# Row statistics taken where a tile is finished, shorter stages between the layers, and two accumulators for the expert outputs

## The reference, cut to what matters

```
x = x + lru(layernorm(x))          # gated complex linear recurrence
x = x + ffn(layernorm(x))          # binarized weight
x = x + ssm(layernorm(x))          # state space scan
x = x + ffn(layernorm(x))          # the same weight again
x = x + attention(layernorm(x))    # 16 heads, x @ Wq.T and so on, out @ Wo.T
x = x + moe(layernorm(x))          # 64 experts, top 8, 256 places each
x = x + linear_attention(layernorm(x))
x = x + moe(layernorm(x))          # the same experts again

layernorm(x)        = (x - mean) / sqrt(var + 1e-5)      # per row
binarize_weight(w)  = (where(w >= 0, 1, -1) * mean(|w|, per row) - w) + w
ffn(x)              = x @ binarize_weight(w).T + bias
moe(x): logits = x @ router.T; the 8 best experts of a row with normalized softmax weights;
        y_row = sum over its experts of weight * (silu(x @ gate) * (x @ up)) @ down
```

## Time and profile before

| | |
|---|---|
| time, median of 3 runs | 5667.46 us (5666.89 to 5673.59) |
| the profiled execution | 5669.14 us, its span 5667.4 us |
| PE busy | 4820.4 us, 85% of the span |
| DVE busy | 2362.7 us, 42% |
| ACT busy | 1644.4 us, 29% |
| POOL busy | 1527.4 us, 27% |
| DMA, mean over the span | 70 GB/s |

### The profile page before, as it was taken

One profiled execution on the slowest core, in us unless ns is written; L12 is line 12 of the kernel. 1 busy time (PEld: TensorE's weight loads), 2 busy tenths in 40 slices (PEclk: granted clock), 3 DMA queues, 4 the chain that ended last, 5 costly groups with the idle time before them and its releaser, 6 DMA issues. The chain is left out here.

```text
span 5667.4 us, 66951 instructions
## 1 busy us (share of the span) xinstructions
PE 4820.4 (85%) x26288; PEld 2581.4 (46%) x26288; DVE 2362.7 (42%) x3233; ACT 1644.4 (29%) x2764; POOL 1527.4 (27%) x951
## 2 busy tenths in 40 slices
PE   6045988789999999985999949999999989589996
PEld 2013433333333333244655626666666654465654
DVE  1754588537666666744211122333333320512111
ACT  2511555120455555732111112222222210211111
POOL 0011000100577777011444430111111110044444
PEclk9567999899999999986999979999999999699998
DMA  1000000000000000013888840000000021368887
GB/s 46 0 9 17 16 0 0 0 32 1 1 1 1 1 1 1 1 55 112 221 224 226 226 87 25 29 23 29 31 29 31 21 101 61 131 172 224 218 225 164
DMA packets 223978, 395.83 MB, mean 70 GB/s; under 512 B 30480, under 2 KB 118544, under 8 KB 223632
## 3 DMA queue, kind: packets, MB, share of 16 engines
q1 hardware_dynamic: 166352, 249.13, 13.1%
q0 software_dynamic: 57344, 142.64, 12.3%
HBM read 288.88 MB, written 107.02 MB: 70 GB/s over the span
## 5 line engine op out<-in xcount | busy, mean ns | idle before, releaser
L2163 PE MATMUL linb_pr_ps<-lin_z,linb_wt 128*128 128x512 f32 x1536 | 677.8, 595 | 16.4 <-POOL linb_slope_own L2133 16.4
L1365 ACT ACTIVATE attc_prob<-attc_ps 128x512 f32<-128x512 f32 x1024 | 549.1, 596 | 443.0 <-PE attc_ps L1276 442.2
L1239 POOL TENSOR_TENSOR attc_acc<-attc_acc,attc_prob 128x2048 f32<-128x2048 f32 x120 | 547.9, 4566 | 121.6 <-ACT attc_prob L1365 109.2
L1389 DVE TENSOR_REDUCE attc_peak<-attc_ps 128x2 f32<-128x1024 f32 x384 | 469.6, 1225 | 258.0 <-PE attc_ps L1284 258.0
L1276 PE MATMUL attc_ps<-att_q,att_k 32*128 32x512 f32 x2048 | 528.6, 616 | 0.0
L1284 PE MATMUL attc_ps<-att_k,att_q 32*128 32x512 f32 x1536 | 450.0, 663 | 0.0
L2163 PEld LDWEIGHTS linb_pr_ps<-lin_z,linb_wt 128*128 128x128 f32 x1536 | 286.1, 191 | 342.1 <-issue 324.8
L2339 DVE SCALAR_TENSOR_TENSOR linb_gated<-linb_osb,linb_norm_w,linb_proj 128x512 f32<-128x512 f32 x64 | 94.4, 1474 | 668.1 <-ACT linb_osb L2266 668.1
L2140 POOL TENSOR_TENSOR linb_sq<-linb_osb 128x512 f32<-128x512 f32 x64 | 70.1, 1095 | 1039.0 <-ACT linb_osb L2266 1039.0
L1297 PE MATMUL attc_ps<-attc_prob,att_v 128*32 128x256 f32 (+1 forms) x3472 | 316.5, 437 | 0.3 <-ACT attc_prob L1365 0.3
L886 DVE TENSOR_TENSOR_SCAN ssmb_state<-ssmb_decay,ssmb_bu 128x2048 f32<-128x2048 f32 x64 | 279.7, 4409 | 78.9 <-ACT ssmb_decay L833 78.9
(11 more groups left out here) (510 smaller groups left out, 7652.8 us busy)
## 6 DMA issues: line engine op xcount, KB each, us to landing
moe1w_wgu<-in_L_ffn_gate_up_proj SPq DMA_DIRECT2D x32, 1536.0 KB
moe2w_wgu<-in_L_ffn_gate_up_proj SPq DMA_DIRECT2D x32, 1536.0 KB
moe1w_wd<-in_L_ffn_down_proj SPq DMA_DIRECT2D x32, 512.0 KB
gated_features<-linb_gated SPq DMA_DIRECT2D x64, 256.0 KB
moe2w_wd<-in_L_ffn_down_proj SPq DMA_DIRECT2D x32, 512.0 KB
linc_gt<-gated_features SPq DMA_DIRECT2D x7, 2048.0 KB
linb_wt<-in_L_attn_b_qkv_w SPq DMA_DIRECT2D x16, 768.0 KB
residual_rows<-residual SPq DMA_DIRECT2D x2, 4096.0 KB
```

Source lines behind the costliest of these rows:

```text
L1239: pool.tensor_tensor(acc[:, n % 2, :, :], before, prob[:, U % NP, :, :], ALU.add).then_inc(pool_done, 2 if at == 1 else 1)
L1365: nc.scalar.activation(prob[:, U % NP, h, :], ps[:, n % 3 if at < 0 else at % 6, :], ACT.Exp).then_inc(exp_done, 1)
L1389: V.tensor_reduce(peak[:, w // TT % 2, i % QH, 2 * hp:2 * hp + 2, b], ps[:, bank:bank + 2, :], axis=AX.X, op=ALU.max).then_inc(mx_used, 1)
L2163: last = nc.tensor.matmul(pr_ps[:, use % 2, :], wt[:, b, kind, k, :], z[:, k, t * NB:(t + 1) * NB], start=(k == 0), stop=(k == DT - 1))
```

## The change

- `g.stats` is a buffer of the whole program. The 16 `bn_stats` leave `Norm`; each is issued on DVE where a tile of `g.X` is finished: while x is loaded (in four DMAs instead of one), after the adds of `lrud`, `ffn1`, `ffn2`, `atte` and `linc`, after the last column block of `ssmb`, and at the end of `moe1c`.
- `project_and_add` has its loops unrolled, reads the features of a tile in place (no copy on ACT), has four PSUM tiles, and PE waits for no bias.
- `lru_outputs` is one stage. `W_out` is loaded during `lruc` into `th[0]`, once `recur(0)` is done. The binarized weight is made within the stage, one DVE step behind each of the first adds, and transposed by PE after tiles 13 and 14.
- To make room in `lruc`, `spare` and `ones` shrink, and `turn` in `gate_and_unwind` works on halves of 1024 columns.
- The ffn bias is loaded in each `ffn` stage.
- The four attention weights come transposed from the host; `attw` is gone, and `atta` loads them.
- Experts 0 and 1 of a pair add to tables of their own, `g.y_dram[0]` and `g.y_dram[1]`; a scatter waits only for the scatters of the same expert number of the pair before. POOL issues the gathers of pair j + 3 ahead of the scatters of pair j - 1, into `NX = 20` buffers. `moe_logits` also writes 4 MB of zeros to the second table. At the end both tables are loaded in four pieces each, DVE sums them, and the second `moe` stores the sums to the output.

```diff
@@ setup @@
+            for j in range(4):
+                sp.dma_start(g.X[:, 4 * j:4 * j + 4, :], ...).then_inc(loaded[j], 16)
...
+        @block.vector
+        def _(dve):
+            for i in range(TT):
+                dve.wait_ge(loaded[i // 4], 16)
+                nc.vector.bn_stats(g.stats[:, i, :], g.X[:, i, :]).then_inc(summed, 1)
@@ Norm.on_vector @@
         for i in range(TT):
-            nc.vector.bn_stats(self.stats[:, i, :], self.X[:, i, :]).then_inc(self.summed, 1)
-        for i in range(TT):
-            dve.wait_ge(self.summed, i + 1)
             nc.vector.bn_aggr(self.mv[:, i, :], self.stats[:, i, :]).then_inc(self.summed, 1)
@@ project_and_add @@
-            pe.wait_ge(loaded, 16)
...
+            for i in range(TT):
+                if i >= NY:
+                    pe.wait_ge(y_used, i - NY + 1)
+                for k in range(DT):
+                    last = nc.tensor.matmul(y_ps[:, i % NY, :], h[:, k, i * P:(i + 1) * P], w[:, k, :], start=(k == 0), stop=(k == DT - 1))
+                last.then_inc(y_ready, 1)
...
+            for i in range(TT):
+                dve.wait_ge(y_ready, i + 1)
+                dve.wait_ge(biased, i + 1)
+                nc.vector.tensor_tensor(g.X[:, i, :], g.X[:, i, :], y_ps[:, i % NY, :], ALU.add).then_inc(y_used, 1)
+                dve.wait_ge(y_used, i + 1)
+                nc.vector.bn_stats(g.stats[:, i, :], g.X[:, i, :]).then_inc(summed, 1)
@@ lru_recurrence @@
+            sp.wait_ge(dve_step, after_vector("recur0"))
+            sp.dma_start(th[0].rearrange("p (k f) -> p k f", f=D), g.dram["L0_attn_a_W_out"].rearrange("(k p) f -> p k f", p=P)).then_inc(w_loaded, 16)
...
-                turn(r, cos_sum[r], sin_sum[r], spare[:, :], gx[r], -1)
+                for c in range(2):
+                    half = slice(c * (T // 2), (c + 1) * (T // 2))
+                    turn(r, cos_sum[r][:, half], sin_sum[r][:, half], spare[:, :], gx[r][:, half], -1, half)
@@ lru_outputs (tensor) @@
+                if i == TT - 3:
+                    pe.wait_ge(bw_ready, 1)
+                    turned(0)
+                    turned(1)
+                elif i == TT - 2:
+                    turned(2)
+                    turned(3)
@@ ffn (vector, in the loop) @@
+                    dve.wait_ge(y_used, i + 3)
+                    dve.sem_inc(passed, 1)
+                    nc.vector.bn_stats(g.stats[:, bass.ds(i, 1), :].rearrange("p o s -> p (o s)"), ...).then_inc(summed, 1)
@@ ssm_scan, add_back @@
+                if e == DT - 1:
+                    dve.wait_ge(added, e * TC + t + 1)
+                    for i in range(t * 4, (t + 1) * 4):
+                        V.bn_stats(g.stats[:, i, :], g.X[:, i, :]).then_inc(stats_ready, 1)
@@ attention @@
-            normalized_features(nc, g, "atta", z)
-            transpose_weights(nc, g, "attw", v, ...)
+            normalized_features(nc, g, "atta", z, tuple(zip(("L1_attn_a_Wq", ...), (*wt, wo))))
@@ moe_logits (sync) @@
+            sp.dma_start(g.y_dram[0][0:T, :].rearrange("(i p) d -> p i d", p=P), g.X[:, :, :]).then_inc(x_saved, 16)
+            sp.wait_ge(blank, 1)
+            for i in range(0, TT, NB_ROWS):
+                sp.dma_start(g.y_dram[1][i * P:(i + NB_ROWS) * P, :].rearrange("(i p) d -> p i d", p=P), nothing[:, :, :]).then_inc(x_saved, 16)
@@ moe_experts @@
-        NX = 16
+        NX = 20
...
+            for r in range(TT // NR):
+                tiles = slice(r * NR, (r + 1) * NR)
+                for to, rows in ((g.X, g.y_dram[0]), (second, g.y_dram[1])):
+                    sp.dma_start(to[:, tiles, :], ...).then_inc(back[r], 16)
+            for r in range(TT // NR):
+                sp.wait_ge(summed, r + 1)
+                if last:
+                    sp.dma_start(g.dram["out"][0, r * NR * P:(r + 1) * NR * P, :]..., g.X[:, r * NR:(r + 1) * NR, :]).then_inc(stored, 16)
...
             def scatter(j, x):
                 mine = [4 * j + 2 * s + x for s in range(2)]
-                others = [4 * j + 2 * s for s in range(2)] if x else [4 * j - 3, 4 * j - 1]
-                for y in others:
-                    if y >= 0:
-                        pool.wait_ge(added[y % NY], 16 * (y // NY + 1))
+                if j >= 1:
+                    for y in mine:
+                        pool.wait_ge(added[(y - 4) % NY], 16 * ((y - 4) // NY + 1))
...
             for j in range(PAIRS):
+                if j + AHEAD < PAIRS:
+                    for n in range(4 * (j + AHEAD), 4 * (j + AHEAD + 1)):
+                        gather(n)
                 if j >= 1:
                     for x in range(2):
                         scatter(j - 1, x)
-                if j + AHEAD < PAIRS:
-                    for n in range(4 * (j + AHEAD), 4 * (j + AHEAD + 1)):
-                        gather(n)
...
+            for r in range(TT // NR):
+                dve.wait_ge(back[r], 32)
+                nc.vector.tensor_tensor(g.X[:, r * NR:(r + 1) * NR, :], ..., second[:, r * NR:(r + 1) * NR, :], ALU.add).then_inc(summed, 1)
+                if not last:
+                    dve.wait_ge(summed, r + 1)
+                    for i in range(r * NR, (r + 1) * NR):
+                        nc.vector.bn_stats(g.stats[:, i, :], g.X[:, i, :]).then_inc(stats_ready, 1)
```

## The result

The changed kernel takes 5481.49 us in the median of 4 runs (5474.49 to 5487.45), beside 5669.05 us for the kernel before (4 runs, 5666.89 to 5673.59). The ratio is 0.9672, with a 95% interval of 0.9658 to 0.9685: faster, by 3.3%. The forecast was 5486 us. The profiled execution has a span of 5480.8 us; before it was 5667.4, so 186.6 us have to be accounted for.

What follows compares the result with a forecast made beforehand. No single engine bounds the whole; POOL's scatter chain through the DMA sets the expert stages. Terms of 220.0 us less and 37.4 more, net -183, take 5669 to 5486 us; 8 in 10 range 5455 to 5535.

Steps and rivals of the forecast that it cites:

- The step that carried half of the sum: Expert stages moe1c and moe2c: POOL's chain through the DMA sets the pace, PE only looks like the bound; -107 us.
- The chain: Expert stages: scatter (0.30 + 1.6 us), landing (8.9), the same for the other expert; about 20 to 21 us a pair.
- rival B: Expert stages: gathers do not come earlier, something unseen holds them, the pace stays 20.5; 5593 us, chance 0.07.
- Rival C: Expert stages: up to four accumulating scatters at once hinder one another, slower than before; 5729 us at 23 a pair, chance 0.03.
- The pace: Middle of moe1c and moe2c: 18.5 us a pair instead of 20.49, ends 18.4 and 19.6; 53.6 us saved in moe1c.
- Rival A: Expert stages: the DMA engines take POOL's place as the bound, 19.2 us a pair; 5524 us, chance 0.20.
- moe1a and moe2a: Routing stages: DVE's tile 4 waits for a store queued behind x and zeros; +5.3 us each, bounds -9.5 to +15.
- Statistics: Six other stages lose 9.51 us of statistics at their head: -57.1 us; they come back where nothing hides them.
- lrud with binarizing: From lruc's end through lrud and binw: 62.7 us instead of 96.0, 33.3 saved, binarizing hidden under PE's products.
- attw: Attention: the stage goes, -18.9 us, and its 4 MB load hides under what is left of atta.
- the ends of the expert stages: Earlier last scatter against loading and adding two tables: +4.3 us for moe1c, +9.5 for moe2c.
- the load of two tables: End of the expert stages: 8 MB instead of 4 MB come, 11.5 us more of data than before.

Runs made afterwards that it cites:

- Run 1: Changed kernel with POOL's old order (scatters ahead of gathers) and 16 gather buffers, the two tables kept: 5470.47 us, ratio 0.9643.
- Run 2: Kernel before with POOL's new order and 20 gather buffers, still one table with chained scatters: 5638.42 us, ratio 0.9939.
- run 8: Changed kernel loading the gate and up weights of each pair's first expert a second time from pair 4 on: 5481.14 us, ratio 0.9666.
- run 9: As run 8, but both experts' gate and up weights are loaded a second time: 5587.55 us, ratio 0.9847.
- run 3: Changed kernel with GpSimd pausing ahead of the ninth gather until the first pair's products have begun: 5469.58 us, ratio 0.9641.
- run 4: Changed kernel with GpSimd's old order but still 20 gather buffers: 5465.74 us, ratio 0.9638.
- run 10: Changed kernel with 28 extra identity products on TensorE behind the product of tile 3 in moe1a and moe2a: 5486.78 us, ratio 0.9672.

## Why the prediction was right, and where it was not

**The bound.** The step that carried half of the sum holds: GpSimd's queue waits in order for landings of its own scatters and sets the pace, while PE looked like the bound. Run 1 cut the chain and left the rest: 18.4 us a pair. Run 2 gave GpSimd a head start and left the chain: the pace went back to 20.5 when the stock was gone.

The chain was drawn one landing too long. Its terms, twice 0.30 + 1.6 + 8.9, make 21.6 us and not "20 to 21", more than the 20.49 found. In the kernel before (GpSimd, timeline; columns as in the earlier trace rows) the second scatter of expert 1 and, four gathers later, the next pair's first scatter are:

```profile
2951.52 1.56 POOL L1864 DMA_INDIRECT residual_rows<-moe1c_ye,moe1w_index  x1 [0.30 <-issue]
2958.50 1.62 POOL L1864 DMA_INDIRECT residual_rows<-moe1c_ye,moe1w_index  x1 [0.30 <-issue]
```

The second may not begin before the first has landed, and it begins after 7.0 us with no idle time beyond the usual 0.30. So this landing took less than 7 us and lay under the four gathers. Only the landing ahead of expert 1's scatters stood open: 8.1 us of idle time in the mean, beside 12.4 us of issuing, 20.5 in all (scatters of pairs 1 to 27). The 8.9 us of the earlier trace rows are those of expert 0's scatters alone, 10 of the 20 in its window. The sum did not suffer, since with the wait gone the pace is PE's 18.4 us however many landings there were; but that the landing times explained the pace "to the microsecond", which the prediction held against rival B, was a coincidence.

Rival B fell with the lead of 33.9 us (I had worked out 40; the pair's results come later in its 18.4 us than I placed them). Rival C fell with up to four scatters at once and pairs of 18.36 us. The second scatter of expert 1 does land later than before, 8.5 us after its issue rather than 5.3 (medians in moe1c, by the semaphore events of the two traces), but nothing waits for it any more.

**The pace: 18.36, not 18.5.** The 0.14 us make 7 us in the sum. I moved off PE's row because 17.8 us of DMA time in 18.5 seemed to leave 4%. That step took DMA share times length as work that must be done. Per pair the same bytes showed 17.8 us before, 16.9 in the changed kernel, and with 17% more bytes 18.7, at no cost. So the share is not work that adds up; it may hold time in which packets wait on one another, which is not shown. Rival A, to which I gave 0.20, put the limit at the door. It lies beyond 291 GB/s, 17% above what the kernel moves (run 8); where, is open, since run 9 lost time partly to a wait of its own. The rate was the better reading: the earlier trace rows shows 233 GB/s in moe1a and the earlier trace rows only 224 in the pairs, and neither was at a limit: the changed kernel moved 314 in moe1a and 248 in the pairs.

**A term left out: the opening of the expert stages, +13 us.** I priced the new order in the middle and not at the start, where it queues 20 gathers ahead of the first scatter rather than 16. PE is then slowed for some 7 us by something that the profile does not name. Runs 3 and 4 show that it follows the burst. It took away twice what the pace had given in addition, and with it the new order as a whole costs time: run 4 without it is 15.7 us faster.

**moe1a and moe2a: the mechanism right, the sum 11 us off.** VectorE's tile 4 is held until a store lands, at +25.6 us (predicted +27.5), and the loads of weights followed at +49.0 in moe2a (predicted +50.0, 5.3 us behind the +44.7 of the earlier trace rows). In moe1a they came at +42.4. The term assumed the half clock of the earlier trace rows for the blocks behind the wait; in moe1a of the changed kernel they ran at the full one:

```profile
2451.23 1.04 PE L1581 MATMUL moe1a_zt_ps<-ident,moe1a_z 128*128 128x128 f32 x8
2452.51 2.00 PE L1589 MATMUL moe1a_lg_ps<-moe1a_rwt,moe1a_zt 128*128 128x64 f32 x16 [0.24 <-ACT moe1a_zt L1607]
```

against 1.91 and 3.68 us a block at the half. Over the profiled runs of kernels whose code is the same here, moe1a took 63.2, twice 67.4 and four times 69.1 to 70.6 us, and moe2a six times 69.2 to 70.2 and once 61.7. Before, the two stages took 66.8 and 66.6 us; in run 2, whose code is the same there, 67.1 and 61.4. So either kernel has two outcomes here, and I had priced only the slower. For that one, too, 5.3 was too much: it cost 2.3 to 3.8 us, and the store landed 1.9 us sooner than I had it.

**The rest.** Statistics, lrud with binarizing, attw, the tails and the ends of the expert stages were each within 2 us. For lruc's halves 2.0 were predicted and 3.1 measured. For ssmb 6.4 and 5.1: there I had put 0.6 us on each statistic and a gap of 0.1, and the five operations took 3.1 us together. For the load of two tables I took 26 us. The Trainium skill (DMA: Bandwidth & Descriptors, Anatomy of one DMA) fits 2.0 us plus bytes by 436 GB/s to one DMA that GpSimd issues, which makes an estimate of 21 us for these 8 MB. The trace, where SyncE issues eight DMAs, has 23.9 from the first issue (3172.34) to the start of the last add (3196.26), between the two. Drift in untouched stages is +5.3 us. The two large misses, -7 for the pace and the 11 of the routing stages on one side, +13 for the openings on the other, cancelled by luck: the total was nearer (4.5 us) than its terms were.

## What to carry to other kernels

Look for the chain behind an engine that seems full: a queue in order that waits for landings of its own transfers shows itself as a transfer which arrives just in time although it was meant to be far ahead, and cutting the chain (a second target, so that nothing waits for the landing) is worth more than a longer head start, which is used up. Look which of its landings stand open as idle time and which lie under other issues, before adding them up. Don't take a DMA share near 1 for the absence of room: ask how many GB/s the same mix has reached, and if nothing shows it, load something twice and see, without giving the extra load a wait of its own. Price a reordered queue at its start and end too, not only in its steady state.

## What the runs showed of the hardware that I had not expected

- **A burst of gathers goes with slow issue on TensorE.** At the start of moe1c, 32 products that take 3.67 us undisturbed took 11.6 us with 20 gathers under way and 5.9 us with 16 (run 4): single products 1.4 us apart, about 1 us idle under "issue". The stutter moved when the gathers were moved (run 3). What the two share is not shown.
- **The DMA share can pass 1 with nothing lost, and be lower where time is lost:** 0.92 at 248 GB/s, 1.02 at 291, and 0.97 at 295 with PE waiting, since there the DMA engines stood idle for 2 to 2.5 us a pair and ran at 1.07 between.
- **A scatter's landing depends on its place.** In moe1c before, the two scatters of expert 0 landed 8.7 and 8.9 us after their issue and those of expert 1 after 4.8 and 5.3 us (medians by the semaphore events), from the same queue. Why is not shown.
- **Short idle times of TensorE went with slower products.** In moe1c before, 34.75 us of waiting went with 22.55 us of slower products at a clock of 0.96; without the waits it was 1.00.
- **The clock behind a gap can come out at either level.** After 12 to 14 us idle, PE worked on at the half clock in one routing stage (0.52 over 62 us) and came to the full clock in the other (0.69), with the same instructions. With 7.4 us of unbroken extra products ahead (run 10) both stages had the full one.
- **One or two hundredths of the clock in a stage of about a millisecond** (attc 998.9 us at 0.98 or 1008.4 at 0.97, linb 1232.4 at 0.99 or 1260.1 at 0.97) weigh as much as most of the edits here.
